# Paired heads and grouped waits for the 64-row matmuls of two attentions, in a transformer layer on eight cores

## The reference

```python
x = x + attn(layernorm(x))                       # attention 1, then Wout
  # scores = clip(q @ k.T * 0.125, -10, 10), causal, softmax, @ v
x = x + ffn(layernorm(x))                        # the rest
  # ac = (q + u) @ k.T
  # bd = rel_shift((q + v) @ r.T)                # r = pe @ Wr, relative positions
  # attn = softmax(causal((ac + bd) * 0.125)); h = LN(x + attn @ v @ Wo)
  # h = LN(h + relu(h @ Wff1) @ Wff2)
  # h = LN(h + gate * expert[argmax](h))         # 8 experts, 1024 -> 4096 -> 1024
  # return h @ Wout
```

## Time and profile before

| | |
|---|---|
| time, median of 3 runs | 8427.95 us (8294.83 to 8759.74) |
| time of the profiled execution | 8294.83 us |
| its span, slowest core (core 2) | 8293.7 us |
| the other cores' spans | 8226.0 to 8281.0 us |
| TensorE (PE) busy | 6275.0 us, 76% |
| weight loads (PEld) | 3528.6 us, 43% |
| ScalarE (ACT), VectorE (DVE) busy | 24%, 21% |
| mean granted TensorE clock, core 2 | 0.813 of 2.4 GHz |

### The profile page before, as it was taken

The page is one execution under the profiler, slowest core; times in us unless marked ns, Lnnn a source line. Parts: engine busy times, 40 slices in busy tenths (PEclk is TensorE's granted clock), DMA queues, the critical chain, the costliest instruction groups (busy, mean ns, idle before and its releaser), DMA issues.

```text
span 8293.7 us, 117794 instructions; the slowest of 8 cores (8226.0 to 8293.7 us)
## 1 busy us (share of the span) xinstructions
PE 6275.0 (76%) x39706; PEld 3528.6 (43%) x39984; DVE 1770.0 (21%) x4261; ACT 1985.6 (24%) x4069; POOL 499.8 (6%) x942
## 2 busy tenths in 40 slices
PE   2867647534589944667699898989989899998954
PEld 1323323100144422344365565655656565565631
DVE  3366432344422115222200000000000000000025
ACT  0145200222244420122122222222222222222210
POOL 0000000121100010000100001010000101001000
PEclk9855678655555557888799999999999999999977
DMA  4000231233355663411602305050230505014012
GB/s 105 8 11 7 78 110 31 97 121 128 95 92 89 107 113 99 92 41 31 109 9 47 54 11 89 9 92 9 35 66 9 92 9 86 15 27 73 9 54 84
DMA packets 582216, 506.58 MB, mean 61 GB/s; under 512 B 376712, under 2 KB 450696, under 8 KB 581648
## 3 DMA queue, kind: packets, MB, share of 16 engines
q0 software_dynamic: 119472, 268.53, 16.4%
q1 hardware_dynamic: 417376, 180.16, 9.6%
q10 hardware_dynamic: 44800, 50.34, 1.7%
HBM read 524.10 MB, written 150.99 MB: 81 GB/s over the span
## 4 chain that ended last, share of the span: by engine, by line
PE 61%; DMA 18%; DVE 10%; issue 7%; ACT 3%; DVEq 1%; SPq 0%; POOL 0%; ACTq 0%; POOLq 0%
PE ps L1132 21%; PE ps L1118 20%; DMA W<-fWe 10%; PE ps L829 5%; DMA bd<-bst 4%; PE ps L840 4%; PE ps L722 3%; PE ps L305 2%; PE ps L774 2%; DVE bst L603 1%; DMA W<-fWff 1%; PE ps L745 1%; PE ps L1066 1%; PE ps L592 1%; PE ps L554 1%
## 5 line engine op out<-in xcount | busy, mean ns | idle before, releaser
L1132 PE MATMUL ps<-W,hidT 128*128 128x512 bf16 x9000 | 2013.6, 383 | 247.6 <-DMA W<-fWe 159.8
L1118 PE MATMUL ps<-mhw,W 128*128 128x256 bf16 x16384 | 1862.1, 272 | 38.9 <-DMA W<-fWe 33.3
L1124 ACT ACTIVATE hidT<-ps,c_be1c 128x256 bf16<-128x256 f32 x2048 | 971.1, 474 | 2920.6 <-PE ps L1118 2918.7
L1118 PEld LDWEIGHTS ps<-mhw,W 128*128 128x128 bf16 x16384 | 1470.8, 97 | 433.3 <-issue 145.0
L1132 PEld LDWEIGHTS ps<-W,hidT 128*128 128x128 bf16 x9216 | 901.8, 99 | 1344.1 <-issue 294.2
L1004 DVE SCALAR_TENSOR_TENSOR msel<-ps,c_maskg,msel 128x512 bf16<-128x512 f32 x256 | 192.1, 751 | 3696.0 <-PE ps L1132 3696.0
L592 PE MATMUL ps<-rT,qv 64*128 64x512 bf16 x640 | 271.0, 597 | 405.2 <-DVE qv L580 286.2
L128 POOL DMA_DIRECT2D W<-fWe x512 | 271.0, 534 | 3864.6 <-PE ps L1118 3350.4
L829 PE MATMUL ps<-qu,KT 64*128 64x512 bf16 (+3 forms) x640 | 340.8, 533 | 45.3 <-DVE qu L800 45.3
L603 DVE CAST bst<-ps 128x512 bf16<-128x512 f32 x384 | 262.7, 691 | 392.8 <-ACT bst L598 159.7
L840 PE MATMUL ps<-c_ident,bdsh 128*128 128x128 bf16 x2176 | 344.1, 303 | 3.1 <-DMA bdsh<-bd 3.0
(11 more groups left out here) (191 smaller groups left out, 3986.2 us busy)
## 6 DMA issues: line engine op xcount, KB each, us to landing
W<-fWe POOLq DMA_DIRECT2D x512, 256.0 KB, 12.7
bdsh<-bd SPq DMA_DIRECT2D x448, 128.0 KB, 3.7
bd<-bst POOLq DMA_DIRECT2D x64, 512.0 KB, 2.9
mhw<-h2T SPq DMA_DIRECT2D x64, 512.0 KB, 4.0
bd<-bst POOLq DMA_DIRECT2D x64, 384.0 KB, 2.6
bd<-bst POOLq DMA_DIRECT2D x64, 256.0 KB, 2.3
W<-fWff POOLq DMA_DIRECT2D x64, 256.0 KB, 13.9
bd<-zfill SPq DMA_DIRECT2D x32, 256.0 KB, 4.6
```

Source lines behind the costliest of these rows:

```text
L1118: k.op("pe", lambda e, fc=fc, dc=dc, psj=psj: e.matmul(self.ps[psj][:, 0:256], W1[:, dc * FF + fc * 128: dc * FF + fc * 128 + 128], hT[:, ...
L1124: k.op("act", lambda e, fc=fc, psj=psj: e.activation(hid[:, fc * 256: fc * 256 + 256], self.ps[psj][:, 0:256], AF.Relu, bias=b1sb[:, boff ...
L1132: k.op("pe", lambda e, fc=fc, t2=t2, dh=dh, psj=psj: e.matmul(self.ps[psj][:, :], hid[:, fc * 256 + t2 * 128: fc * 256 + t2 * 128 + 128], ...
```

## The change

`K.waits_for` emits an operation's waits without the operation, and `op(..., nowait=True)` an operation without its waits. With these, each of the three stages first makes the waits of several matmuls and then issues the matmuls in one run, so that those of the two heads stand side by side.

- bd stage: the loop over chunks is now outside the loop over heads. Per chunk: the waits of both heads, both matmuls, then both copies; head 0's copy goes to ScalarE for even chunks, head 1's for odd ones, and the other to VectorE. Both stores come after the last chunk.
- Attentions: blocks are taken in groups of three. A group makes the waits for its six banks, issues its six score matmuls, and (attention 2) makes the waits for its six `bdsh` buffers and issues all their identity matmuls; the exps and what follows come last. The loads of the group stand at its start, and `bdsh` is used modulo 3 in place of 4.

```diff
+    def waits_for(self, e, reads=(), writes=()):
+        for t in self._dep_toks(reads, writes):
+            self._wait(e, t)
...
-                for h in range(2):
-                    head = 2 * hp + h
-                    r0 = h * 64
-                    b, Bb = bst[h]
-                    for jc in range(jc_min, TC):
+                for jc in range(jc_min, TC):
+                    for h in range(2):
                         psj = h * 2 + (jc % 2)
+                        k.waits_for("pe", reads=[Bq, BrTl[hp]],
+                                    writes=[self.Bps[psj]])
+                    for h in range(2):
...
-                        if jc % 2 == 0:
+                            nowait=True)
+                    for h in range(2):
+                        psj = h * 2 + (jc % 2)
+                        b, Bb = bst[h]
+                        if (jc + h) % 2 == 0:
...
+                for h in range(2):
+                    head = 2 * hp + h
+                    b, Bb = bst[h]
+                    njc = TC - jc_min
                     k.dma("pool",
...
-                for sc in range(tcc * 4 + 4):
...
+                sc_max = tcc * 4 + 4
+                for g0 in range(0, sc_max, 3):
+                    scg = range(g0, min(g0 + 3, sc_max))
                     if bd:
+                        for sc in scg:
...
-                            w, Bw = self.bdsh[h][sc % 4]
+                                w, Bw = self.bdsh[h][sc % 3]
+                                k.dma("sp", w[:, 0:nj * 128],
...
+                    for sc in scg:
+                        c0 = max(0, sc - tcc * 4) * 128
+                        for h in range(2):
+                            psj = h + (sc % 3) * 2
+                            qd = qdep if qdep is not None else BQTl[hp]
+                            k.waits_for("pe", reads=[BKTl[hp], qd],
+                                        writes=[self.Bps[psj]])
...
+                                inc=not bd, nowait=True)
+                    if bd:
+                        for sc in scg:
...
+                                k.waits_for("pe", reads=[Bw, self.Bp["ident"]],
+                                            writes=[self.Bps[psj]])
```

More of the change, by code:

```diff
@@ L91, in _dep_toks, with op @@
         return toks
-    def op(self, e, fn, reads=(), writes=(), inc=True):
+    def waits_for(self, e, reads=(), writes=()):
         for t in self._dep_toks(reads, writes):
             self._wait(e, t)
+    def op(self, e, fn, reads=(), writes=(), inc=True, nowait=False):
+        if not nowait:
+            for t in self._dep_toks(reads, writes):
+                self._wait(e, t)
         instr = fn(self.eng[e])
@@ new lines, in attention @@
+                    if bd:
+                        for sc in scg:
+                            jmin = max(0, sc - tcc * 4)
+                            for h in range(2):
+                                psj = h + (sc % 3) * 2
+                                w, Bw = self.bdsh[h][sc % 3]
+                                k.waits_for("pe", reads=[Bw, self.Bp["ident"]],
+                                            writes=[self.Bps[psj]])
+                        for sc in scg:
+                            jmin = max(0, sc - tcc * 4)
+                            for h in range(2):
+                                psj = h + (sc % 3) * 2
+                                w, Bw = self.bdsh[h][sc % 3]
+                                for j in range(jmin, 4):
+                                    k.op("pe", lambda e, j=j, jmin=jmin, psj=psj,
+                                         w=w: e.matmul(
+                                        self.ps[psj][:, j * 128:(j + 1) * 128],
+                                        w[:, (j - jmin) * 128: (j - jmin) * 128 + 128],
+                                        self.sb_p["ident"][:, :],
+                                        start=False, stop=(j == 3)),
+                                        reads=[Bw, self.Bp["ident"]],
+                                        writes=[self.Bps[psj]], inc=(j == 3),
+                                        nowait=True)
```

119 lines of the change are left out of this document (57 added, 62 removed).

## The result

After: 8690.2 us median of 13 executions (8509.8 to 9174.0). Before, with 13 executions by then: 8514.2 us (8294.8 to 9004.2). The ratio is **1.025, interval 1.020 to 1.030**: slower. The profiled execution went from 8294.8 to 8509.8 us, +215 where I forecast +182.

The account below looks back on a forecast made before the run. It took ScalarE's exps to bound attention 1, the staging buffer's store loop bd, and TensorE attention 2, with 41% of the span in untouched dense layers. 8294.8 + 59 + 61 + 62 gave 8477 us, range 8330 to 8650.

Parts of the forecast that it names:

- the slow loads: Rival in attention 2: six bias loads take 9.3 us to land, adding 174 us, 8589 us in all; chance 0.15.
- the forecast's own upper part: Top of the forecast's own range of 8410 to 8560 us, with attention 2 at up to +140 us.
- The bd term: bd stage: both stores issued at the end, the store's round trip no longer hidden by the other head; +61 us.
- The rule of program order: bd, width 2: VectorE's queue holds head 1's first copy ahead of head 0's second, delaying head 0; +0.75 us per tile.
- head 1's lag: bd: head 1's staging buffer comes free about 0.8 us after head 0's, 1.1 for 512 KB stores.
- My upper end of +90: High end for the bd stage, if both stores slow each other down as much again.
- Attention 1: Group barrier over six banks leaves ScalarE standing, 0.98 us lost per boundary; +59 us.
- The 44 us for a full clock: Attention 1's cost if the matmul at a boundary runs at full clock, some 0.78 us lost per boundary.
- Attention 2: Three bias buffers per head and waits for all six loads make loads the limit, 8.2 us per group; +62 us.
- Loads land in time: Rival: attention 2 runs at TensorE's 5.5 us per group and gives back 90 us, 8325 us in all; chance 0.22.
- Pairs not side by side: Rival in bd and attention 2: a weight load between paired matmuls costs 0.43 us per pair, 8531 us; chance 0.06.
- The barriers cost nothing: Rival in the three stages: bd lag absorbed and copies halved (-60), loads in time (-90), 8204 us; chance 0.07.

Follow-up runs that it names:

- experiment 4: Kernel after, with head 0's bd copies all on VectorE and head 1's on ScalarE; bd stage 731 to 747 us.
- experiment 5: Kernel after, without the joint wait in bd, each matmul waiting for its own bank; bd stage 744 to 752 us.
- experiment 6: Kernel after, without the joint wait in bd and with each head's copies on its own engine; bd stage 682 to 686 us.
- experiment 1: Kernel after, with groups of one block in both attentions and four bias buffers per head; attention 2 636 to 660 us, whole 8223.6 us.
- experiment 2: Kernel after, with six bias buffers per head in place of three, groups of three kept; attention 2 690 to 704 us, whole 8332.9 us.
- experiment 9: Kernel after, with groups of one block, four bias buffers per head and own waits per matmul in the attentions; attention 2 734 to 745 us.
- experiment 10: Kernel of experiment 9 without head 1's first bias matmul waiting for head 0's last one to finish; attention 2 638 to 668 us.
- experiment 11: Kernel after, with groups of one block, eight bias buffers per head and four bst tiles; 7822.0 us profiled, ratio to before 0.939.

## Why the prediction was wrong, point by point

The direction, the three mechanisms in the main and the profiled time (33 us off) held; the time of 8690.2 lies above my upper end of 8650. The 33 us are the 35 by which `bd` cost more than forecast, less 11 in attention 2, and some 10 from outside the three stages. These are means: in attention 2 the single cores miss by -25 (core 2) to +21 us (core 4), so part of the closeness is luck.

*The step that failed: the range's upper end.* I added the costs to the profiled execution. That the median of the three runs lay 133 us above it I noted, but the range has no term for it. With 13 executions each, the medians lie 180 us (after) and 219 us (before) above the profiled ones; with every stage as forecast, 8477 + 180 = 8657 would have been out of the range already. The upper end came from the slow loads (8589) and a little, "the more so as a median can lie above"; it should have been the forecast's own upper part plus that distance: 8560 + 180 is 8740. Even the 133 us that the prediction itself states would have done: 8560 + 133 is 8693.

*The bd term, 61 forecast, 96 measured.* By widths 1 to 4 I had 0, +0.75, +0.65 and +0.9 us per tile; core 2 shows -0.2, +0.7, +1.2 and +1.5 (5.14, 6.8, 8.1 us after). The rule of program order held where it was tested alone (experiment 4, width 2). The term was mis-sized in two ways: I took 0.8 to 1.1 us as head 1's lag, where at width 4 it is 0.55 for the issue plus 0.8 for the slower second landing (medians 3.78 against 2.97 us), 1.35 in all; and I costed head 0 as free of head 1's banks at widths 3 and 4, which experiments 4, 5 and 6 contradict: only with both ties cut do 84 of the 96 us come back (some of it may be the copying of two heads side by side, which no run separates). My upper end of +90 lay just short.

*Attention 1, +59 forecast, +59 measured.* From exp to exp the boundary took 1.53 us against 1.47, and experiment 1 takes the whole away. The split holds too: for 4, 8, 12 and 16 blocks I had 0, 8, 20 and 31 us, and the means of the cores grew by 0, 9, 21 and 30. (The 44 us for a full clock is a slip: 7.5 x 8 x 0.78 is 47.)

*Attention 2, +62 forecast, +51 measured* (37 on core 2, 83 on core 4). The mechanism (three buffers, no load ahead) is what experiment 2 shows: six buffers take away 182 us on the mean of the cores. For 4, 8, 12 and 16 blocks I had -7, +2, +18 and +50 us; the means of the cores are -4, +2, +16 and +37, so it is the phases of 16 blocks that I had too long. In the one shown, the loops of 8.06, 7.13 and 7.50 us stand against three of 8.2, and 6.59 against 6.9. The clock is now and then at its upper level (0.63 in the last chunk, above); how much of the 13 us is the clock and how much the loads was not separated.

*The rivals.* "Loads land in time" is what experiment 2 made true, and it showed my price for it too small: I had attention 2 at -90 us, it went to 695, -131. I had priced a group at 5.5 us, at the half clock; at the clock that experiment 2 was granted it takes 4.49. (15 groups of 0.8 us in 8 pairs are 96 us, not 90.) From the fit that the Trainium skill (DMA: Bandwidth & Descriptors, Anatomy of one DMA) gives for the software path I estimate about 2.3 us for a load of 128 KB. The profile books these loads to `hardware_dynamic`, not to the software queue. The quickest of a burst agrees with the 2.3 us, but the trace differs for the others: the median from issue to landing in the kernel after is 3.5 us, with the loads in bursts of six. "Pairs not side by side" is out: two score matmuls of 0.61 us take 0.61 together (experiment 9). "The barriers cost nothing" is out by experiments 1 and 2; its 8204 still had the 59 us of attention 1 in it, and without them would have been 8145.

*What I did not see at all* is that the order costs or frees so much in attention 2. I let TensorE's loop fall from 6.5 to 5.5 us per group of three blocks, 0.33 us a block, where 0.66 was to be had at the same clock, and took the half clock as given.

## What to carry to other kernels

To run two row groups of the array side by side it was enough here that their matmuls stand next to each other in the queue (experiments 9 and 10). A group barrier over many banks is no part of it, and each one cost the consumer a refill (exp to exp 1.53 us instead of 0.47). Before grouping, count the buffers: with as many tiles as one group waits for, no load can be ahead; twice as many cut TensorE's wait from 175 to 12 us (experiment 2). Where two streams are merged into one loop, look for every tie through which the early one waits for the late one (joint waits, shared copy engines, one issuing queue), since cutting a single one may show next to nothing.

## What the runs showed of the hardware that I had not expected

*The granted clock changed with the order of the work.* TensorE's timeline, attention 2, of before:

```profile
2745.51 0.61 PE L829 MATMUL ps<-qu,KT 64*128 64x512 bf16 x1
2746.05 0.61 PE L840 MATMUL ps<-c_ident,bdsh 128*128 128x128 bf16 x4
2746.59 0.61 PE L829 MATMUL ps<-qu,KT 64*128 64x512 bf16 x1
2747.13 0.61 PE L840 MATMUL ps<-c_ident,bdsh 128*128 128x128 bf16 x4
2747.67 0.61 PE L829 MATMUL ps<-qu,KT 64*128 64x512 bf16 x1
```

and of experiment 11, where the clock happens to rise:

```profile
2423.80 0.61 PE L857 MATMUL ps<-qu,KT 64*128 64x512 bf16 x2
2424.34 1.04 PE L879 MATMUL ps<-c_ident,bdsh 128*128 128x128 bf16 x8
2425.30 0.61 PE L857 MATMUL ps<-qu,KT 64*128 64x512 bf16 x2
2425.85 0.67 PE L879 MATMUL ps<-c_ident,bdsh 128*128 128x128 bf16 x8
2426.45 0.39 PE L857 MATMUL ps<-qu,KT 64*128 64x512 bf16 x2
2426.77 0.62 PE L879 MATMUL ps<-c_ident,bdsh 128*128 128x128 bf16 x8
2427.32 0.39 PE L857 MATMUL ps<-qu,KT 64*128 64x512 bf16 x2
```

Both heads of a block take 2.16 us before (2745.51 to 2747.67), 1.50 in the new order at 1.2 GHz (2423.80 to 2425.30) and 0.87 at 2.4 GHz (2426.45 to 2427.32). The first step is the order: 0.66 us over the 224 blocks of full width is 148 us, an estimate of what it is worth at the lower clock. The second is the clock. Before had TensorE at work almost all the time and stayed at the lower level, here in the windows row of its third chunk (230 of 248 us busy, clock 0.50):

```profile
2450.69:2698.41 247.72, 229.96 (x1536) 115.35 (x1536) 49.04 (x202) 104.31 (x192) 2.14 (x4) 0.50 0.55 95
```

The new order, busy for less of the time (161 of 228 us in the last chunk of experiment 1), had 0.91. The Trainium skill (TensorE: Matmul & The Clock Gate, Part 1: The HAM clock gate) says that the default is the throttled clock and activity releases it; by busy time the kernel before should then have had the higher clock, and these rows differ. They don't decide what the chip goes by: the kernel before was busy for more of the time but took longer for the same matmuls, and a higher clock shortens busy time by itself. Nor is it settled what in the order lifts the clock. Experiment 9, with one short stop in the middle of each block, got 0.67, and 10, which differs in that stop alone, 0.86; so it isn't the joint wait. Without the waits for loads it rose as well (0.63 after, 0.85 in experiment 2, one order).

*TensorE waiting for its own result cost 0.30 us* (1.34 against 1.04 us for the same eight matmuls, at 1.2 GHz), and attention 2, with the lower clock that came with it, 84 us (738 against 654, mean of the cores, experiments 9 and 10).

*Two stores issued together slowed almost the second only*: medians of 2.97 and 3.78 us at width 4, 0.55 us apart, against 2.90 and 2.99 when they lay 2.36 us apart in the kernel before (core 2).
